# Columns of the shared tiles by block loads and a VectorE transpose, with tile partitions in sample order and the row shift in two parts

## The reference

```python
s0 = relu(x @ swi[0]) @ swo[0];  s1 = relu(x @ swi[1]) @ swo[1]
eo = relu(x @ wi[type]) @ wo[type]
w  = softmax(relu(concat(eo[:,0], s0[:,0], s1[:,0]) @ g1) @ g2)
x  = x + eo*w[:,0] + s0*w[:,1] + s1*w[:,2]
# y = x seen as (sample, 64 rows, 256 columns); reflect at both borders
x  = x + zX*(left - 2y + right) + zY*(row above - 2y + row below) + zR*y*(1-y)
```

## Time and profile before

| | |
|---|---|
| median of three runs | 1192.49 us (1191.89 to 1193.87) |
| the profiled execution, its own time | 1192.88 us |
| its span, first to last instruction | 1191.0 us |
| PE busy / weight loads busy | 98% / 83% of the span |
| DVE / ACT / GpSimd busy | 56% / 39% / 6% |
| DMA, mean over the span | 82 GB/s |
| packets under 512 B | 8368 of 39041 |

### The profile page before, as it was taken

The page is one execution under the profiler, slowest core; times in us unless marked ns, Lnnn a source line. Parts: engine busy times, 40 slices in busy tenths (PEclk is TensorE's granted clock), DMA queues, the critical chain, the costliest instruction groups (busy, mean ns, idle before and its releaser), DMA issues.

```text
span 1191.0 us, 16700 instructions
## 1 busy us (share of the span) xinstructions
PE 1164.8 (98%) x6124; PEld 992.0 (83%) x6124; DVE 672.7 (56%) x1008; ACT 460.2 (39%) x802; POOL 72.5 (6%) x105
## 2 busy tenths in 40 slices
PE   5999999999999999999999999999999999999995
PEld 4888888888889998888888888888888888888884
DVE  6655555555557763555555565465465465465455
ACT  3445444444545652332423333333333233333232
POOL 3101110110112200000000000000000000000001
PEclk9999999999999999999999999999999999999998
DMA  7644453444446633022022022021021021021110
GB/s 230 182 124 129 145 152 111 145 148 129 118 140 187 218 109 93 10 54 62 5 58 63 1 62 54 9 63 45 18 62 45 18 63 45 18 63 36 27 27 27
DMA packets 39041, 98.09 MB, mean 82 GB/s; under 512 B 8368, under 2 KB 15536, under 8 KB 38960
## 3 DMA queue, kind: packets, MB, share of 16 engines
q1 hardware_dynamic: 26720, 52.98, 16.3%
q0 software_dynamic: 12096, 44.05, 12.5%
q10 hardware_dynamic: 144, 0.00, 0.0%
HBM read 75.24 MB, written 17.56 MB: 78 GB/s over the span
## 4 chain that ended last, share of the span: by engine, by line
PE 95%; DVE 2%; DMA 1%; SPq 1%; issue 0%; ACT 0%; DVEq 0%; ACTq 0%
PE acc L717 31%; PE acc L718 15%; PE hbank L693 15%; PE hbank L692 15%; PE hbank L694 15%; PE tbank L656 2%; DMA g1s<-in_L_cond_g 1%; PE tbank L657 1%; DMA xs<-in_x 0%; SPq L915 0%; SPq L903 0%; PE acc L706 0%; PE tbank L664 0%; DVE rows L350 0%; DMA itk<-in_itok_B 0%
## 5 line engine op out<-in xcount | busy, mean ns | idle before, releaser
L471 DVE SCALAR_TENSOR_TENSOR hl<-hbank,hh 128x512 fp32r<-128x512 f32 (+1 forms) x424 | 278.0, 656 | 437.9 <-ACT hh L781 437.7
L781 ACT ACTIVATE hh<-hbank 128x512 fp32r<-128x512 f32 (+1 forms) x424 | 241.6, 570 | 621.0 <-PE hbank L694 617.3
L717 PE MATMUL acc<-swo,hh 128*128 128x512 f32 x1024 | 370.9, 396 | 0.0
L718 PE MATMUL acc<-swo,hl 128*128 128x256 f32 x1024 | 286.9, 280 | 0.0
L717 PEld LDWEIGHTS acc<-swo,hh 128*128 128x128 f32 x1024 | 192.3, 188 | 45.5 <-DVE eo L489 0.2
L717 PE MATMUL acc<-ewo,hh 128*128 128x512 f32 x560 | 205.1, 397 | 0.2
L692 PE MATMUL hbank<-xh,swh 128*128 128x512 f32 x512 | 204.8, 400 | 0.0
L693 PE MATMUL hbank<-xl,swh 128*128 128x512 f32 x512 | 202.2, 395 | 0.0
L718 PEld LDWEIGHTS acc<-swo,hl 128*128 128x128 f32 x1024 | 193.1, 189 | 10.0
L694 PE MATMUL hbank<-xh,swl 128*128 128x512 f32 x512 | 199.7, 390 | 0.0
L718 PE MATMUL acc<-ewo,hl 128*128 128x256 f32 x560 | 157.3, 281 | 0.0
(11 more groups left out here) (164 smaller groups left out, 873.7 us busy)
## 6 DMA issues: line engine op xcount, KB each, us to landing
rw<-in_L_cond_wi POOLq DMA_DIRECT2D x42, 512.0 KB, 4.4
rw<-in_L_cond_wo POOLq DMA_DIRECT2D x42, 512.0 KB, 5.3
xs<-in_x SPq DMA_DIRECT2D x140, 64.0 KB, 2.9
eo_scratch<-eo SPq DMA_DIRECT2D x140, 64.0 KB, 2.7
xs<-in_x SPq DMA_DIRECT2D x16, 512.0 KB, 5.2
ei<-eo_scratch SPq DMA_DIRECT2D x16, 512.0 KB, 6.6
out<-ot SPq DMA_DIRECT2D x15, 512.0 KB, 3.8
y<-y SPq DMA_DIRECT2D x32, 120.0 KB
```

The lines of the kernel that those rows point to most:

```text
L471: e.scalar_tensor_tensor(HL[:, g % NH, 0:w], bank[:, 0:w], 0.0, HH[:, g % NH, 0:w].bitcast(F32), ALU.max, ALU.subtract).then_inc(h_lo, 1)
L717: e.matmul(acc[j][:, 0:2 * D], HH[:, g % NH, js], woc[:, c, :], start=(c == 0), stop=False)
L718: m = e.matmul(acc[j][:, D:2 * D], HL[:, g % NH, js], woc[:, c, 0:D], start=False, stop=last)
L781: e.activation(HH[:, g % NH, 0:w], hbank[g % HRING][:, 0:w], ACT.Relu).then_inc(h_hi, 1)
```

## The change

For the 16 shared tiles the PE transposes, their bank copies and their DVE remainders go. SP loads a second copy of x for each tile (`load_tile_blocks`): 16 transfers of 32 partitions x 8 runs x 32 elements, so that DVE can turn all 32x32 blocks with one `transpose` of 128x1024 (`turn_tile`, in chunk 4 of the pass ahead). The loads go to `XB`, two of the buffers that held raw expert weights; the turned tile goes to `XZ`, a third. ACT copies it whole to `XH` in chunk 4 (`tile_high_whole`), DVE writes `XL` whole in chunk 5 (`tile_low_whole`). In `XH` and `XL` the two feature halves now alternate in runs of 128 columns, so the first product of a shared pass reads its 512 columns as four runs (`tile_cols`). The expert passes keep their PE transposes.

Partitions of a tile now go sample by sample (16 four-row groups each). The row shift is one step of a partition, done as parts of 112 and 15 partitions (`shifted`); then, after a wait for these, two transfers of 8 partitions put in the reflected rows (`reflected`). `lap_y` waits for six transfers. The pattern `b8`, which spreads the gate values, follows the new order.

```diff
 def tile_parts(n, c):
-    if n == 0 or n >= NP - 2 or (PASSES[n][0] == SH and PASSES[n][1] % 2 == 0):
+    if n == 0 or n >= FIRST - 1:
         return []
     tile = tile_of(n) + 1
-    big = tile <= NBIG or tile > NU
+    big = tile <= NBIG
     if c == 4:
         return [(tile, 0 if big else None)]
     return [(tile, 1)] if c == 5 and big else []
...
+def next_tile(n, c):
+    if c != 4 or n < FIRST - 1 or n >= NP - 2:
+        return None
+    if n == FIRST - 1:
+        return 0
+    t, b = PASSES[n][1] // 2, PASSES[n][1] % 2
+    return t + 1 if b == 1 else None
...
-        XH = [sb(f"xh{i}", [128, 2, 512], F32R) for i in range(2)]
-        XL = [sb(f"xl{i}", [128, 2, 512], F32R) for i in range(2)]
+        XH = [sb(f"xh{i}", [128, 1024], F32R) for i in range(2)]
+        XL = [sb(f"xl{i}", [128, 1024], F32R) for i in range(2)]
...
+        XB, XZ = RW[0:2], RW[2]
+        def unit_cols(a):
+            return a[:].rearrange("p (k n) -> p k n", k=2)
+        def tile_cols(a, k):
+            return a[:].rearrange("p (j k n) -> p j k n", j=4, k=2)[:, :, k, :]
...
         def out_rows(a, t):
-            return a[8 * t:8 * t + 8, :, :].rearrange("b (p j) d -> p b (j d)", j=4)
+            return a[8 * t:8 * t + 8, :, :].rearrange("b (p j) d -> (b p) (j d)", j=4)
...
+            def turn_tile(t):
+                if t == 0:
+                    e.wait_ge(*cut_done(1 + NU, 2))
+                else:
+                    e.wait_ge(xt_lo, t)
+                e.wait_ge(xb_in[t % 2], 256 * (t // 2 + 1))
+                e.transpose(XZ[:], XB[t % 2][:]).then_inc(xz_done, 1)
+            def tile_low_whole(t):
+                tile = 1 + NU + t
+                e.wait_ge(xt_hi, t + 1)
+                e.tensor_tensor(XL[tile % 2][:], XZ[:], XH[tile % 2][:].bitcast(F32), ALU.subtract).then_inc(xt_lo, 1)
...
             def lap_y(t):
                 y = Y[t % 2]
-                e.wait_ge(halo_in[t % 2], 64 * (t // 2 + 1))
+                e.wait_ge(halo_in[t % 2], 96 * (t // 2 + 1))
                 e.wait_ge(dve_seq, V.n)
...
+                    if next_tile(n, c) is not None:
+                        turn_tile(next_tile(n, c))
+                    if next_tile(n, c - 1) is not None:
+                        tile_low_whole(next_tile(n, c - 1))
...
-                xh, xl = XH[tile % 2], XL[tile % 2]
-                if c == 0:
-                    e.wait_ge(t_free, T_AT[tile_last(tile)])
+                if PASSES[n][0] == EXP:
+                    xh, xl = ([unit_cols(a[tile % 2])[:, k, 0:w] for k in range(2)] for a in (XH, XL))
+                    to = bank[:, 0:w]
+                    if c == 0:
+                        e.wait_ge(t_free, T_AT[tile_last(tile)])
+                else:
+                    xh, xl = ([tile_cols(a[tile % 2], k) for k in range(2)] for a in (XH, XL))
+                    to = bank[:].rearrange("p (j n) -> p j n", j=4)
+                    if c == 0:
+                        e.wait_ge(xt_lo, PASSES[n][1] // 2 + 1)
...
                 for k in range(2):
-                    e.matmul(bank[:, 0:w], wh[:, k, cs], xh[:, k, 0:w], start=(k == 0), stop=False)
-                    e.matmul(bank[:, 0:w], wh[:, k, cs], xl[:, k, 0:w], start=False, stop=False)
-                    i = e.matmul(bank[:, 0:w], wl[:, k, cs], xh[:, k, 0:w], start=False, stop=(k == 1))
+                    e.matmul(to, wh[:, k, cs], xh[k], start=(k == 0), stop=False)
+                    e.matmul(to, wh[:, k, cs], xl[k], start=False, stop=False)
+                    i = e.matmul(to, wl[:, k, cs], xh[k], start=False, stop=(k == 1))
                 i.then_inc(h_prod, 1)
...
+            def tile_high_whole(t):
+                tile = 1 + NU + t
+                e.wait_ge(xz_done, t + 1)
+                e.wait_ge(h_prod, (LAST_PASS[tile - 2] + 1) * NC)
+                e.activation(XH[tile % 2][:], XZ[:], ACT.Copy).then_inc(xt_hi, 1)
...
             def load_tile_x(t):
                 tile = 1 + NU + t
-                e.wait_ge(t_prod, T_AT[tile_last(tile - 2)])
-                if t >= 2:
+                if t < 2:
+                    e.wait_ge(t_prod, T_AT[tile_last(tile - 2)])
+                else:
                     e.wait_ge(dve_seq, AT["residual", t - 2])
...
+            def load_tile_blocks(t):
+                if t == 0:
+                    e.wait_ge(*cut_done(1 + NU, 0))
+                if t == 1:
+                    e.wait_ge(*cut_done(1 + NU, 1))
+                if t >= 2:
+                    e.wait_ge(xz_done, t - 1)
+                to = XB[t % 2][:].rearrange("p (j n) -> p j n", n=128)
+                for q in range(4):
+                    rows = x[8 * t + 2 * q:8 * t + 2 * q + 2, :, :].rearrange("b (m j) (k d) -> (b m) (j k) d", j=4, k=2)
+                    for a in range(4):
+                        e.dma_start(to[32 * a:32 * a + 32, :, 32 * q:32 * q + 32],
+                                    rows[:, :, 32 * a:32 * a + 32]).then_inc(xb_in[t % 2], 16)
...
+            def shifted(t):
+                y = Y[t % 2]
+                for a, b in ((0, 112), (112, 127)):
+                    e.dma_start(y[a + 1:b + 1, 0, :], y[a:b, 4, :]).then_inc(halo_in[t % 2], 16)
+                    e.dma_start(y[a:b, 5, :], y[a + 1:b + 1, 1, :]).then_inc(halo_in[t % 2], 16)
             def halos(t):
+                e.wait_ge(dve_seq, AT["shared", t, 1])
+                shifted(t)
+            def reflected(t):
                 y = Y[t % 2]
-                e.wait_ge(dve_seq, AT["shared", t, 1])
-                e.dma_start(y[8:128, 0, :], y[0:120, 4, :]).then_inc(halo_in[t % 2], 16)
-                e.dma_start(y[0:120, 5, :], y[8:128, 1, :]).then_inc(halo_in[t % 2], 16)
-                e.dma_start(y[0:8, 0, :], y[0:8, 2, :]).then_inc(halo_in[t % 2], 16)
-                e.dma_start(y[120:128, 5, :], y[120:128, 3, :]).then_inc(halo_in[t % 2], 16)
+                e.wait_ge(halo_in[t % 2], 96 * (t // 2) + 64)
+                e.dma_start(y[0:128:16, 0, :], y[0:128:16, 2, :]).then_inc(halo_in[t % 2], 16)
+                e.dma_start(y[15:128:16, 5, :], y[15:128:16, 3, :]).then_inc(halo_in[t % 2], 16)
...
+                if u == NU - 1:
+                    load_tile_blocks(0)
...
             load_tile_eo(0)
             load_tile_x(1)
+            load_tile_blocks(1)
             load_tile_eo(1)
             for t in range(1, NT):
                 halos(t - 1)
+                reflected(t - 1)
                 if t + 1 < NT:
+                    load_tile_blocks(t + 1)
                     load_tile_x(t + 1)
                     load_tile_eo(t + 1)
...
             t = NT - 1
-            y = Y[t % 2]
             e.wait_ge(dve_seq, AT["last", 3])
-            e.dma_start(y[8:128, 0, :], y[0:120, 4, :]).then_inc(halo_in[t % 2], 16)
-            e.dma_start(y[0:120, 5, :], y[8:128, 1, :]).then_inc(halo_in[t % 2], 16)
+            shifted(t)
             e.wait_ge(dve_seq, AT["last", 1])
-            e.dma_start(y[0:8, 0, :], y[0:8, 2, :]).then_inc(halo_in[t % 2], 16)
             e.wait_ge(dve_seq, AT["last", 2])
-            e.dma_start(y[120:128, 5, :], y[120:128, 3, :]).then_inc(halo_in[t % 2], 16)
+            reflected(t)
             for a in range(2):
                 e.wait_ge(dve_seq, AT["result", t, a])
-                e.dma_start(out_rows(out, t)[:, :, 2 * a * D:(2 * a + 2) * D],
+                e.dma_start(out_rows(out, t)[:, 2 * a * D:(2 * a + 2) * D],
```

More of the change, by code:

```diff
@@ L235, in cond_resid_program @@
         w_lo_pool = sem("w_lo_pool")
+        xb_in = [sem(f"xb_in{i}") for i in range(2)]
+        xz_done = sem("xz_done")
+        xt_hi = sem("xt_hi")
+        xt_lo = sem("xt_lo")
         x_in = [sem(f"x_in{i}") for i in range(2)]
@@ L410, in tile_low @@
             def tile_low(tile, k):
-                hi, lo = XH[tile % 2], XL[tile % 2]
+                hi, lo = unit_cols(XH[tile % 2]), unit_cols(XL[tile % 2])
                 e.wait_ge(t_hi, XT_AT[tile, k])
@@ L764, in tile_high @@
             def tile_high(tile, k):
-                hi = XH[tile % 2]
+                hi = unit_cols(XH[tile % 2])
                 e.wait_ge(t_prod, T_AT[tile, k])
@@ L825, in _ @@
                         tile_high(tile, k)
+                    if next_tile(n, c) is not None:
+                        tile_high_whole(next_tile(n, c))
                 if (n, c) == (FIRST + 1, 0):
@@ L856, in _ @@
                             pattern=[[-1, 128]], channel_multiplier=1).then_inc(consts, 1)
-            e.iota(b8[:], [[0, 16], [1, 8]], base=0, channel_multiplier=0,
+            e.iota(b8[:], [[1, 8], [0, 16]], base=0, channel_multiplier=0,
                    allow_small_or_imprecise_dtypes=True).then_inc(consts, 1)
```

## The result

The changed kernel takes 1182.83 us (median of four, 1181.57 to 1183.5); the kernel before took 1193.18 us beside it. The ratio is 0.9913, with a 95% interval of 0.9895 to 0.993. The forecast was 1181.4 us, the range 1178 to 1190.

The account below looks back on a forecast made before the run. The prediction took the PE, busy for 98% of the span, as the bound. Removed transposes (-14.8 us) plus costs of 2.2, 0.5 and 1.0 gave -11.1, so 1181.4 us at the runs' median, range 1178 to 1190.

Parts of the forecast that it names:

- PE transposes, tiles 1 to 15: Shared passes: removing the transposes gives back 0.91 us of PE time for each of 15 tiles, 13.7 us.
- PE transposes, tile 0: Pass 22, a pass of small chunks: removing tile 0's two transpose groups gives back 1.1 us of PE time.
- tile 0's late block loads: Pass 22: DVE waits 1.9 us for the loads, stalling the PE 2.2 us once, between 0.3 and 6.
- gate weights: PE's wait for `g1s`: its load comes later in SP's queue order, costing 0.5 us, between 0 and 3.
- tail: Last `lap_y`: the reflected transfers land at 1185.8, adding 1.0 us to the path, between 0.4 and 2.5.
- The main term: Shared passes, tiles 1 to 15: PE time of the removed transposes, 13.7 us saved.
- What DVE and ACT got in its place: Chunk 4 of shared passes: block transpose, taken at 1.2 us, and ACT's whole copy cost 0 up to 3.2 us of transpose.
- the 2.1 us in hand: Chunk 4 of shared passes: `hidden_low` is ready at 713.9, and the PE wants it at 716.0.
- The block loads of a tile: SP's queue, shared tiles: 16 loads 0.65 us apart land at H + 17.6, wanted at H + 25.2; hidden, 7.6 us in hand.
- The rival that took twice 52 ns for a packet of 128 bytes: SP and DMA engines, every tile: block loads late, slower from 1.3 us pace, about 1262 us at 1.6; chance 0.12.
- Four runs: Shared matmuls: reading 512 columns as four runs slows 1536 matmuls; 7.2 ns each eats the 11.1 us; chance 0.07.

Follow-up runs that it names:

- order_only: Kernel before with the new partition order, row shift in parts of 112 and 15, PE transposes kept, no block loads; 1193.17 us, ratio 1.0003.
- turn2: Changed kernel with the block transpose of each tile done twice; 1184.07 us, measured once.
- turn3: Changed kernel with the block transpose of each tile done three times; 1193.1 us, measured once.
- tile0_c5: Changed kernel with tile 0's transpose one chunk later, in chunk 5 of pass 22; 1183.69 us, measured once.
- extra16: Changed kernel with 16 additional block loads ahead of each tile's own, from tile 2 on, into an unread buffer; 1196.35 us, measured once.
- both: Changed kernel with tile 0 turned by the PE and, for the last tile, ACT's queue issuing the two shift transfers into slot 5; 1180.36 us, ratio 0.9889.

## Why the prediction was right, point by point

The span's -10.6 us, by stages against the terms of the sum:

| term | forecast | measured | from |
|---|---|---|---|
| PE transposes, tiles 1 to 15 | -13.7 | -13.4 | C to D |
| PE transposes, tile 0 | -1.1 | -1.1 |; inside A to B |
| tile 0's late block loads | +2.2 | +4.1 | A to B: +2.97, and the 1.1 |
| gate weights | +0.5 | -0.4 | B to C |
| tail | +1.0 | +0.5 | D to E +1.39, E to F -0.9 |
| start to A, the same work | 0 | -0.3 | differs from run to run |
| sum | -11.1 | -10.6 | |

The sum lies half a microsecond from the measured one, and part of that is luck: tile 0 came 1.9 us dearer than forecast, and the gate weights, the tail and the start together 1.7 us cheaper. The main term alone missed by 0.3. The mechanism was right for the main term and for what was hidden, and without the three cheaper terms the time would still lie in the range. In the table the 1.1 us of tile 0's transposes is read from the kernel before in both columns; measured is its difference from the stall, A to B's +2.97.

*The main term.* Read from start to start, 0.91 us a tile; 13.4 / 15 = 0.89 came back, with nothing in its place. Shown by `order_only`, which keeps the transposes and gains nothing, and by the changed kernel's full table.

*What DVE and ACT got in its place* was hidden, with the 2.1 us in hand that the prediction worked out: `turn2` and `turn3` lie on its two sides.

*The block loads of a tile* were hidden. Their pace is 0.70 us, where 0.65 was taken. The cover was 0.9 us larger than stated. "710.29 + 16 x 2.785" took the next transpose as one transpose-free period on; but the transposes that vanish lay between 710.29 and H, not between H and the next tile, so 45.48 - 19.32 = 26.16 was right. And the engines were never near: from 733.5 to 743.5 us of the changed kernel

```profile
q1 hardware_dynamic: 3884, 0.47, 30.6%
```

3884 packets were busy for 30.6% of 160 us (10 us of 16 engines), 12.6 ns each. That lies outside the 28 to 52 ns between which the prediction put it, because the 28 was misread: it is 0.6 us x 16 / 342, the time in which packets passed and not the time for which they were busy. By the busy share in the same row, 29.4%, a packet there took 8 ns. The rival that took twice 52 ns for a packet of 128 bytes was eight times too dear. The Trainium skill, "DMA: Bandwidth & Descriptors", Specifications, sets 512 bytes as the least for full rate. The trace agrees as far as it goes: 128 bytes in 12.6 ns are 10 bytes for each busy ns, and the 1 KB in 52 ns of the earlier trace rows, which go from SBUF to SBUF, are 20. It did not matter, since SP's issues set the pace.

*Tile 0* is the term that was mis-sized: 2.2 us forecast, 4.1 measured. The place was right and DVE's wait near (2.8 us, 1.9 forecast; the pace of 0.70 makes most of it). The PE's wait was 2.7 us from start to start (2.5 as the profile lists it). What was missing is the clock: after the wait, matmuls ran at 1.2 GHz from 444.87 to 447.60, 2.7 us, worth the other 1.4. The prediction charged waits at their length.

*The gate weights* went the other way, because the new order, which I had put down as changing no size on the engines, shortened the transfers around them (`order_only` has the same 0.35 us). The same holds for E to F in *the tail*: the forecast had the later landing of the reflected rows (1.0 forecast, 1.39 measured: they are issued at 1172.77, 2.1 us after the fourth shift issue, not 1.6), and missed the quicker last store.

*Four runs* cost nothing: shared matmuls start at 701.30 and 701.53, 0.23 us apart, as before, and C to D came within 0.3 us of the forecast, 0.2 ns for each of the 1500 or so in it. That rival has a slip in its price: at 14 ns each, 1536 matmuls are 21.5 us and the time would be 1203, not 1192; 1192 is where its 7.2 ns lead.

## What to carry to other kernels

Work taken off a full PE comes back at its start-to-start cost, if what replaces it fits the lag between producer and consumer; compute that lag in microseconds. Here doubling and tripling the new work met it to a tenth. The steady state may be covered while the first use is not, because there the buffers come free late: look at the first tile by itself, and keep the old way for it when the load cannot come sooner. Charge a PE wait of a few microseconds with the slow matmuls behind it, and compare stages between marks, not spans, for anything below 2 us.

## What the runs showed of the hardware that I had not expected

- The PE's granted clock was 0.57 in the mean of four microseconds after a wait of 2.5 us (changed kernel), and 0.57 after one of 1.7 us (`tile0_c5`). After one of 5.0 us (`turn3`) the matmuls ran at 1.2 GHz for 5.6 us. After 14 waits of about 1 us (`extra16`) and 14 of 0.5 us (`turn3`) it stayed 1.00. No run separates the length of the wait from the smaller matmuls around pass 22.
- A packet of 128 bytes from HBM was busy for 12.6 ns, and a load of 256 of them cost SP 0.61 us of issue, 0.70 from one to the next, with the engines busy for 31%.
- 512 KB of tile rows with eight samples interleaved on the partitions took 5.2 us to load and 3.8 to store; sample by sample, 3.7 and 2.7 (`order_only`). In the changed kernel the stores took 6.2 us, right behind the loads of the next tile, and nothing waited for them.
- Two DMA issues on ACT's queue beside two on SP's held ACT for 2.27 us; SP's same two shapes took 1.44, as long as alone. Of ACT's two, the one of 15 partitions took 1.60 us and the one of 112 took 0.63 (`both`).
